# Router product and three up projections of the last feed-forward issued inside the attention stream

## The reference, cut to what matters

```python
gate = xt @ wg                               # router logits, 8 experts
top_val, top_idx = jax.lax.top_k(gate, 4)
gs = jax.nn.softmax(top_val, axis=-1)
gs_eff = jnp.ones_like(gs) + gs - stop_gradient(gs)
h = jax.nn.relu(jnp.einsum('nd,ehd->neh', xt, w1))     # "up", all 8 experts
out_all = jnp.einsum('neh,eoh->neo', h, w2)            # "down"
out = jnp.einsum('nk,nko->no', gs_eff, take(out_all, top_idx))
# x = x + 0.5 * out;   attn1 before it ends with: out @ w_o.T
```

## Time and profile before

| | us |
|---|---|
| median of 3 runs | 561.94 (561.33 to 562.6) |
| profiled execution | 559.89 |
| its span, first to last instruction | 558.2 |
| PE, DVE, ACT, POOL busy in the span | 509.4, 391.7, 264.4, 126.4 |

### The profile page before, as it was taken

One profiled execution on the slowest core, in us unless ns is written; L12 is line 12 of the kernel. 1 busy time (PEld: TensorE's weight loads), 2 busy tenths in 40 slices (PEclk: granted clock), 3 DMA queues, 4 the chain that ended last, 5 costly groups with the idle time before them and its releaser, 6 DMA issues.

```text
span 558.2 us, 9242 instructions
## 1 busy us (share of the span) xinstructions
PE 509.4 (91%) x3106; PEld 433.9 (78%) x3106; DVE 391.7 (70%) x1196; ACT 264.4 (47%) x572; POOL 126.4 (23%) x201
## 2 busy tenths in 40 slices
PE   1999999999999999999999969998589988889996
PEld 1788888888888888888888858886477776668885
DVE  3669786763886754976687878687177876737775
ACT  2557543443334353235553263574446766644441
POOL 1001000110100100100010054355325554414342
PEclk9999999999999999999999997999668999889999
DMA  6332310000000000002100003302827330000011
GB/s 196 89 107 78 95 39 1 0 1 1 2 1 0 2 1 0 2 21 63 32 0 2 2 1 110 89 1 104 167 79 237 89 84 2 1 1 1 1 39 38
DMA packets 16734, 24.83 MB, mean 44 GB/s; under 512 B 2736, under 2 KB 11184, under 8 KB 16592
## 3 DMA queue, kind: packets, MB, share of 16 engines
q1 hardware_dynamic: 15632, 23.73, 14.6%
q10 hardware_dynamic: 1056, 0.51, 0.4%
HBM read 18.99 MB, written 5.24 MB: 43 GB/s over the span
## 4 chain that ended last, share of the span: by engine, by line
PE 78%; DVE 6%; issue 6%; ACT 4%; POOL 4%; DMA 1%; ACTq 1%; DVEq 0%; POOLq 0%
PE ps L573 22%; PE ps L575 21%; PE ps L574 20%; PE ps L888 2%; PE ps L588 2%; DVE x L1590 2%; PE ps L842 2%; PE ps L855 2%; PE ps L874 1%; PE ps L872 1%; POOL al L506 1%; PE ps L959 1%; ACT z L995 1%; PE ps L840 1%; DMA post_b<-in_posts_dram 1%
## 5 line engine op out<-in xcount | busy, mean ns | idle before, releaser
L573 PE MATMUL ps<-zh,w0u_h 128*128 128x512 f32 x256 | 103.2, 403 | 2.5 <-issue 2.5
L575 PE MATMUL ps<-zl,w0u_h 128*128 128x512 f32 x256 | 102.6, 401 | 0.0
L574 PE MATMUL ps<-zh,w0u_l 128*128 128x512 f32 x256 | 102.1, 399 | 0.0
L1025 ACT ACTIVATE gel<-ps 128x512 f32<-128x512 f32 x64 | 38.2, 597 | 104.7 <-PE ps L575 104.5
L1408 DVE TENSOR_TENSOR act<-gel,ps 128x512 f32<-128x512 f32 x64 | 43.8, 684 | 43.5 <-ACT gel L1025 43.3
L573 PE MATMUL ps<-w0d_h,ah 128*128 128x256 f32 x256 | 73.1, 285 | 0.4
L575 PE MATMUL ps<-w0d_l,ah 128*128 128x256 f32 x256 | 71.5, 279 | 0.0
L574 PE MATMUL ps<-w0d_h,al 128*128 128x256 f32 x256 | 71.5, 279 | 0.0
L506 POOL TENSOR_TENSOR al<-act,ah 128x512 fp32r<-128x512 f32 x32 | 42.2, 1319 | 82.8 <-ACT ah L1102 82.6
L1590 DVE SCALAR_TENSOR_TENSOR x<-ps,aff,x 128x256 f32<-128x256 f32 x128 | 53.0, 477 | 9.9 <-PE ps L575 8.1
L573 PEld LDWEIGHTS ps<-zh,w0u_h 128*128 128x128 f32 x256 | 48.8, 191 | 13.8 <-issue 4.4
(11 more groups left out here) (183 smaller groups left out, 1110.8 us busy)
## 6 DMA issues: line engine op xcount, KB each, us to landing
stage<-in_w_dram SPq DMA_DIRECT2D x16, 384.0 KB, 3.1
q_raw<-split_out SPq DMA_DIRECT2D x24, 128.0 KB, 2.8
k_raw<-split_out SPq DMA_DIRECT2D x48, 64.0 KB, 2.7
stage<-in_w_dram SPq DMA_DIRECT2D x8, 256.0 KB, 2.6
k_raw<-in_zeros_dram SPq DMA_DIRECT2D x1, 1536.0 KB, 11.0
x<-in_x_dram SPq DMA_DIRECT2D x2, 512.0 KB, 5.2
split_out<-qh SPq DMA_DIRECT2D x4, 256.0 KB, 2.1
split_out<-ql SPq DMA_DIRECT2D x4, 256.0 KB, 2.5
```

The costliest lines, as they stand in the source:

```text
L573: pe.matmul(o, lh, rh, start=start, stop=False, **kw)
L574: pe.matmul(o, ll, rh, start=False, stop=False, **kw)
L575: return pe.matmul(o, lh, rl, start=False, stop=stop, **kw)
L1025: nc.scalar.activation(gel[:, n % 2, :], ps[:, 2 * (n % 2), :], ACT.Gelu_apprx_tanh).then_inc(gelu_s, 1)
```

## The change

Three steps of the stream, 70, 71 and 73, get one up projection each (units 16, 17, 18); step 70 also gets `logits_t` ahead of it. Each comes behind whatever else its step has. ACT follows one step later with the copy of the transposed logits and the relus. DVE's `z_lo` moves from the head of the block to step 67. After the stream PE does both `out_back`, up 19, both `out_turn`, `logits`, both `out_project`, down 16, then up and down in turns with the down three units behind. For units from 16 on the raw relu goes to `q_raw` and not to `act32`, and the first of them waits for tile (2, 1)'s projection (`y_ps` at 6), which used the slots. DVE's order for everything but `z_lo` is untouched, as is ACT's `exps` at unit 2, which now comes ahead of the relu of unit 19 only.

```diff
+UP_STEPS = (70, 71, 73)
...
+        hid = [act32[:, i, :] for i in range(2)] + [q_raw[:, i, 0:2, :].rearrange("p a q -> p (a q)") for i in range(2)]
...
+        def hidden(n):
+
+            return hid[n // (2 * U1) * 2 + n % 2]
...
+                    if c == 0 and before(st, b) == "attn1":
+                        pool.wait_ge(y_ps, 6)
+                    nc.gpsimd.tensor_tensor(al[:, slot, :], hidden(n), ah[:, slot, :].bitcast(F32),
...
+                    if before(st, b) == "attn1":
+                        block_start(st, b)
+                        out_back(3, 0)
+                        out_back(3, 1)
+                        up1(first + 3)
+                        out_turn(3, 0)
+                        out_turn(3, 1)
+                        logits(3, routed["ffn1", fb])
+                        out_project(3, 0)
+                        out_project(3, 1)
+                        down1(first)
+                        for c in range(4, U1):
+                            up1(first + c)
+                            down1(first + c - 3)
+                        down1(first + U1 - 3)
+                        continue
...
+                    if s == UP_STEPS[0]:
+                        split_ready(p + 2)
+                        pe.wait_ge(exp_s, 4 * HEADS - 1)
+                        logits_t(1, 3, False)
+                        pe.wait_ge(sht_s, HEADS)
+                    if s in UP_STEPS:
+                        up1(U1 * st.d1 + UP_STEPS.index(s))
...
+                        if not (after_attn1 and c < len(UP_STEPS)):
+                            relu(n)
...
+            def relu(n):
+                act.wait_ge(h1_s, n + 1)
+                if n >= NA:
+                    act.wait_ge(down1_s, n - NA + 1)
+                if n >= 2:
+                    act.wait_ge(al1_s, n - 1)
+                elif n == 0 and f0:
+                    act.wait_ge(al_s, U0 * f0)
+                if n == 2 * U1:
+                    act.wait_ge(y_ps, 6)
+                nc.scalar.activation(hidden(n), ps[:, n % 3, :], ACT.Relu)
+                nc.scalar.activation(ah[:, (U0 * f0 + n) % NA, :], ps[:, n % 3, :], ACT.Relu).then_inc(ah1_s, 1)
...
+                    if s == UP_STEPS[0] + 1:
+                        logits_t_out(routed["ffn1", st.d1], 3)
+                    if s - 1 in UP_STEPS:
+                        relu(U1 * st.d1 + UP_STEPS.index(s - 1))
...
-                            z_lo(p + b)
+                            if not after_attn1:
+                                z_lo(p + b)
...
+                    if s == Z_STEP + 1:
+                        z_lo(p + 2)
```

More of the change, by code:

```diff
@@ L505, in hidden_lo @@
                         pool.wait_ge(down1_s, n - NA + 1)
-                    nc.gpsimd.tensor_tensor(al[:, slot, :], act32[:, n % 2, :], ah[:, slot, :].bitcast(F32),
+                    if c == 0 and before(st, b) == "attn1":
+                        pool.wait_ge(y_ps, 6)
+                    nc.gpsimd.tensor_tensor(al[:, slot, :], hidden(n), ah[:, slot, :].bitcast(F32),
                                             ALU.subtract).then_inc(al1_s, 1)
@@ L695, in ffn1 @@
                 for b in range(2):
+                    fb, first = k + b, U1 * (k + b)
+                    if before(st, b) == "attn1":
[14 more added lines that the diff above has]
+                        continue
                     for c in range(U1):
-                        n, fb = U1 * (k + b) + c, k + b
-                        last_out = before(st, b) == "attn1"
                         if c == 0:
                             block_start(st, b)
[L701 to L704, removed]
+                            split_ready(st.p + b)
                             if before(st, b) == "ffn0":
@@ L727, in ffn1, with up1 @@
                         if c >= LAG:
-                            down1(n - LAG)
+                            down1(first + c - LAG)
+            def up1(n):
+                c = n % U1
+                if n < U1:
+                    pe.wait_ge(w_hi, U0 + c + 1)
+                    pe.wait_ge(w_lo, U0 + c + 1)
+                if n >= 3:
+                    pe.wait_ge(ah1_s, n - 2)
+                for kc in range(KC):
+                    mm = split3(ps[:, n % 3, :], w1_h[:, c, kc * P:(kc + 1) * P], w1_l[:, c, kc * P:(kc + 1) * P],
+                                zh[:, kc, :], zl[:, kc, :], kc == 0, kc == KC - 1)
+                mm.then_inc(h1_s, 1)
             def down1(n):
@@ L1083, in ffn1 @@
                         n, fb = U1 * (k + b) + c, k + b
+                        after_attn1 = before(st, b) == "attn1"
                         if c == 0:
                             left_hi(st, b)
-                            if before(st, b) != "attn1":
-                                z_hi(p + b)
-                            if before(st, b) == "attn1":
+                            if after_attn1:
                                 out_hi(3, 0)
                                 out_hi(3, 1)
[L1091 to L1102, removed]
+                            else:
+                                z_hi(p + b)
+                                logits_t_out(routed["ffn1", fb], 3)
+                        if not (after_attn1 and c < len(UP_STEPS)):
+                            relu(n)
                         if c == (1 if before(st, b) == "ffn0" else 2):
```

## The result

The changed kernel takes 564.14 us (median of 20 runs, 561.97 to 570.08); the kernel before took 561.17 beside it (20 runs, 559.46 to 567.02). The ratio is 1.0065, 95% interval 1.0042 to 1.0088: slower by 3.7 us, between 2.4 and 4.9. The two medians are 2.97 apart. The profiled execution took 564.46, its span 562.7. A second comparison later, `after_again`, gave 1.0038 (1.0009 to 1.0066), which is 2.1 us (0.5 to 3.7).

The account below looks back on a forecast made before the run. DVE's router work, not PE's products, was taken to decide when the last block begins. Later routing, a shorter cast and a second hold gave 4.0 us at accumulation 16, 3.55 after POOL's slack: 561.94 + 3.55 is 565.5 us, range 563.0 to 567.0.

Parts of the forecast that it names:

- my first rival: In the router chain, fewer holds of DVE by POOL: transposition +2.55 us, 564.5, or 563.6 with none; chance 0.27.
- Steps 1 to 4: Stream's end to router chain: 0.50 us wait goes, waits of 0.7 and 0.8 come, `take_logits` 3.5 us later.
- Step 5: DVE's waits for POOL within the router chain: cast shorter, L1355 held again, one successor held 1.0; accumulation 16 4.0 later.
- the cast's saving: In the router chain after `take_logits`, cast L1342 finds POOL idle and saves 0.55 us.
- Step 6: From accumulation 16 to the last block: statistics shift 4.0 us, POOL's scale and the transposition 3.55, nothing given back later.
- My rival of a falling clock: New waits of 2.1 and 1.6 us bring a low-clock slice, costing about 2 us more: 567.5; chance 0.08.
- PE's own waits as the only cost: At the seam, only PE's new waits 0.7 and 0.8 less the removed 0.5 count: +1.0 us, 562.9; chance 0.08.
- Faster: At the seam, halves and additions hide and only removed waits remain: 560.6 to 561.4 us; chance 0.10.

Follow-up runs that it names:

- after_again: The changed kernel run again unedited, against the kernel before in a later session: 564.07 us, ratio 1.0038.
- one_up_in_stream: The changed kernel with one up projection in the stream (unit 16, step 70), not three, and downs two units behind: 562.19 us, ratio 1.0022 to the kernel before.
- up20_covers: The changed kernel with up 20 between logits and the late projections and down 17 right behind down 16: 566.89 us, ratio 1.0093 to the kernel before.
- low19_after_weights: The changed kernel with POOL's low half of unit 19 waiting until the expert weights are ready: 563.59 us, ratio 1.0036 to the kernel before.
- third_low_after_weights: The kernel before with POOL's low half of every ffn1 block's third unit waiting for the expert weights: 562.56 us, ratio 1.0018.
- route_in_stream_stats3: The changed kernel with logits and top-4 work moved into the stream and the second block's statistics two units earlier: 561.57 us, ratio 1.0018 to the kernel before.
- route_only_stats3: Against the changed kernel: no ups in the stream, routing there instead, downs two units behind, statistics two units earlier: 562.41 us, ratio 1.0036 to the kernel before.

## Why the prediction was right, point by point

The direction and the mechanism held: the routing came later behind the late additions, and the last block with it. That the size came out as well (3.55 us for 3.7) is partly luck. My seam was 1 us too long, and 3.7 is a loose number: the medians differ by 2.97, `after_again` gives 2.1, the top level 2.7. The 565.5 also stood on 561.94, the median of three runs; twenty gave 561.17. What happened in the seam, 2.55, is what my first rival had, to which I gave 0.27.

*Steps 1 to 4 held.* The 0.50 wait went, the 1.81 hole stayed, `z_lo` cost nothing (the hole is as long as before). New waits 0.47 and 0.60 for my 0.7 and 0.8. `take_logits` came 13.12 us after the projection in `after_again`, 9.76 before: 3.36 later for my 3.5. one_up_in_stream and up20_covers shift it about as the step says (2.07 for 2.4, 0.89 for 0.95), and the time goes the same way.

*Step 5 was mis-sized.* I had the cast's saving right (0.73 to 0.18) and said that L1355 would be held again and one of its successors as well. L1355 (now L1389) was free: by the code the relu of 19 needs the slot that down 16 frees, which I had not followed, so POOL's low half of 19 began 3.0 us after `take_logits` (514.46 and 511.46) and not 2.3, and L1389 at 2.6 had passed. The hold fell on L1361 (now L1395), by the low half of 19 and not of 20. One hold, where I had two: accumulation 16 came 2.96 later relative to the projection (18.25 for 15.29), not 4.0. That the hold exists is shown twice, by low19_after_weights and third_low_after_weights, which only move POOL's instruction. The SBUF page of the Trainium skill ("SBUF — State Buffer", Who interferes with whom) adds that "Issue order, not op shape, decides who blocks". The trace agrees: the same instruction took 0.19 us where POOL came later and 1.12 where POOL's low half had started 0.23 before it.

*Step 6 was incomplete.* The transposition came 2.55 later at full clock (my rival with fewer holds had 2.55), 0.4 of the chain's delay taken up at POOL as I had it. But I put all of it on the routing. The runs show two chains: the routing, and the downs, which feed accumulation 18 and the statistics behind it. Down 16 starts 13.22 us after the projection, 11.16 before: 2.1 later, behind one more up (1.4) and the waits of 0.47 and 0.60, less the removed 0.50. I had that 2.1 in my own times (510.0 for 507.91) and did not follow it further. With the downs' chain left 1.7 of the 2.7 us stays, with the routing's 2.0; route_in_stream_stats3 removes both and is back at the kernel before. The other premise, that the old waits of 0.21 and 0.59 end by the routing, held for the first only: third_low_after_weights removes the 0.21, and the 0.59 was paced by POOL's low half of unit 21.

*What my sum had not.* At the top level the change costs 2.7 us (2.55 in the seam). The 20 runs gave 3.7, with an interval from 2.4 that includes it. If the other microsecond is real it may lie in the runs with a low clock: 7 of these 20 runs were at the top level (561.97 to 563.39) and six at 0.954 or under, with 566.8 to 570.1; the clocks of the kernel before beside them are not on record. My rival of a falling clock named the new waits (and read one slice at 0.6 where the page has two); the profile has the low clock in the router products, ahead of them, and the old order has it at that place as well. That the change lowers the clock more often is not shown.

*The rivals.* PE's own waits as the only cost: out, by up20_covers, where the first of them is covered and the kernel is 2.5 us slower. Faster: out. Fewer holds: this is what happened in the seam.

## What to carry to other kernels

Work moved ahead of the tail of a stream is also work put in front of that tail: before filling a 0.5 us wait, list what the tail releases (here the additions, and behind them in DVE's order the whole routing) and ask who waits for it last. An order deeper by one unit delays every result of the late half, so what hangs on those results in another engine's program order, here statistics whose input had long been final, must be moved too. Where the levels of the granted clock are worth more than the change, compare kernels at the same level and keep all runs in sight, since a change may itself move runs from one level to another.

## What the hardware showed that I had not expected

Mean granted clock comes in few levels run by run. In the session of `after_again` the kernel before took 559.7 to 560.6 at 0.965, 561.6 to 562.2 at 0.956 and 566.9 to 567.6 at 0.951: more than the change is worth. In the session of one_up_in_stream, on another chip, it took 563.5 and 564.1 at 0.950, so the level does not fix the time. The low stretch moves between executions of one kernel: 498 to 501 in one profile of the changed kernel, 490 to 494 in the next. In the 14 profiles it lies in one of two places, some 4 to 9 us ahead of tile (2, 1)'s projection (five profiles) or around the projection (nine), and both places occur in the old order and in the new.

A DVE instruction of 32 elements with two inputs in SBUF took 0.19 us alone and 0.87 to 1.27 when it came behind the start of a POOL low half (0.87 in one_up_in_stream, 1.27 in route_only_stats3), and in each of these rows it ended 0.04 to 0.06 us after that one, and two could be held one after the other (L1397 and L1408 of up20_covers, 1.15 each).
